# One table word in place of two for TensorE's steps in the building stage of a graph kernel

## The reference

```python
x = x + attention(h, src, dst)          # scores, exp, weighted segment sums, layernorm
x = x + graph_conv(h, src, dst)         # degree-normalised segment sum, one weight
x = x + message_mlp(h, edge_attr, ...)  # two edge MLPs, segment sums to both ends
x = x + gated(h, src, dst, edge_type)   # four GRU steps over segment_sum(msgs, dst)
```

## Time and profile before

| | |
|---|---|
| median of 3 runs | 15553.18 us (15549.36 to 15561.5) |
| the profiled execution | 15585.08 us, span 15583.4 us |
| tables, until the first step | 332 us |
| building stage | 3702 us |
| attention to the end | 11549 us |
| TensorE busy over the span | 72% |

### The profile page before, as it was taken

How to read it: one execution, slowest core, us unless ns; L and a number is a source line. 1 busy time by engine, 2 the same in 40 slices (tenths; PEclk the granted TensorE clock), 3 DMA queues, 4 the chain that set the end, 5 groups by cost and what they waited for, 6 DMA issues and landing times.

```text
span 15583.4 us, 278381 instructions
## 1 busy us (share of the span) xinstructions
PE 11255.6 (72%) x60408; PEld 6377.3 (41%) x60409; DVE 6103.9 (39%) x28509; ACT 3526.9 (23%) x9549; POOL 4597.2 (30%) x4343
## 2 busy tenths in 40 slices
PE   2444444444699976677677677777669999999999
PEld 2222222222222235555555555555554444444443
DVE  6667666766444424333333333333330000000000
ACT  0333333333222202222222222222210000000000
POOL 2000000000000006888888888888800000000000
PEclk7665665665699988999999999999959999999999
DMA  2222222222211152333333333333359989899888
GB/s 92 88 87 87 87 87 91 87 87 87 84 67 71 71 240 36 41 41 41 41 41 41 41 42 41 42 41 41 41 51 345 342 332 341 322 349 342 331 339 305
DMA packets 1120442, 2096.49 MB, mean 135 GB/s; under 512 B 372941, under 2 KB 982880, under 8 KB 1012496
## 3 DMA queue, kind: packets, MB, share of 16 engines
q1 hardware_dynamic: 823736, 1913.57, 34.9%
q0 software_dynamic: 295904, 174.34, 10.9%
HBM read 1630.27 MB, written 457.23 MB: 134 GB/s over the span
## 4 chain that ended last, share of the span: by engine, by line
PE 45%; issue 25%; POOL 14%; DVE 10%; ACT 2%; DMA 1%; DVEq 1%; SPq 1%; POOLq 0%; another core or an unknown queue 0%; ACTq 0%
PE ps L1465 14%; POOL G L488 7%; PE ps L1470 7%; PE ps L1127 7%; POOL reverse L811 5%; DVE hots L1790 3%; PE ps L1182 2%; PE ps L1173 2%; DVE hots L1788 2%; DVE hots L1789 2%; DVE weighed L1864 1%; PE ps L1407 1%; ACT expo L860 1%; DMA reverse<-SD,sidx 1%; PE ps L1268 1%
## 5 line engine op out<-in xcount | busy, mean ns | idle before, releaser
L1127 PE MATMUL ps<-hots 128*128 128x392 f16 x4859 | 1698.6, 453 | 2003.8 <-issue 1751.6
L811 POOL DMA_INDIRECT reverse<-SD,sidx x1660 | 2653.7, 1599 | 389.5 <-issue 380.5
L1465 PE MATMUL ps<-chunk,feat 128*128 128x512 f16 (+1 forms) x10192 | 2279.0, 375 | 14.4 <-DVE feat L2136 13.5
L841 ACT ACTIVATE stagebuf<-ps 128x392 f32 x3248 | 1447.3, 504 | 2288.9 <-PE ps L1130 2234.2
L488 POOL DMA_INDIRECT G<-h_table,idx x1660 | 1652.5, 995 | 493.0 <-issue 484.4
L1127 PEld LDWEIGHTS ps<-hots 128*128 128x128 f16 x4859 | 640.9, 132 | 2779.3 <-issue 2699.8
L1990 DVE TENSOR_TENSOR acc<-acc,ps 128x132 f32 x1660 | 485.4, 292 | 3147.1 <-PE ps L1331 3049.5
L1328 PE MATMUL ps<-MS,OH 128*128 128x128 f32 x3320 | 779.0, 318 | 1263.7 <-issue 791.1
L1788 DVE TENSOR_SCALAR hots<-count_lo,key_lo 128x128 f16<-128x128 f16 x4859 | 1196.0, 246 | 1127.4 <-PE ps L1130 1127.4
L1465 PEld LDWEIGHTS ps<-chunk,feat 128*128 128x128 bf16 x10192 | 943.1, 98 | 1342.7 <-issue 349.5
L1790 DVE TENSOR_SCALAR hots<-count_hi,key_hi 128x294 f16<-128x294 f16 x4859 | 1410.9, 290 | 0.0
(11 more groups left out here) (413 smaller groups left out, 15175.6 us busy)
## 6 DMA issues: line engine op xcount, KB each, us to landing
chunk<-adj SPq DMA_DIRECT2D x720, 1792.0 KB, 9.0
adj<-stagebuf SPq DMA_DIRECT2D x406, 784.0 KB, 5.3
chunkA<-adj SPq DMA_DIRECT2D x48, 1792.0 KB, 6.7
chunk<-adj SPq DMA_DIRECT2D x60, 1232.0 KB, 6.4
G<-in_edge SPq DMA_DIRECT2D x1660, 32.0 KB
G<-h_table,idx POOLq DMA_INDIRECT x1660
reverse<-SD,sidx POOLq DMA_INDIRECT x1660
reverse<-acc SPq DMA_DIRECT2D x4, 3225.0 KB, 20.0
```

The source lines that it names most:

```text
L811: nc.gpsimd.indirect_dma_start(reverse[j % R], bass.IndirectOffsetOnAxis(sidx[:, j:j + 1], 0), SD[:, j % R, :], None, compute_op=ALU.add). ...
L841: nc.scalar.activation(stagebuf[:, bass.ds(held["word"][j] >> ENDBITS, SLEN)].rearrange("p (x c) -> p x c", c=BLK)[:, :, 0:2], bank[j % 8] ...
L1127: nc.tensor.matmul(ps[:, bass.ds(held["to"][j % STEPW], 2 * COMBS)], hots[:, j % BRING, 0:P], hots[:, j % BRING, P:P + 2 * COMBS], start=F ...
L1465: nc.tensor.matmul(bank[k % 2][:, 0:cols], feat[0][:, hi, 0:2, :].rearrange("p a d -> p (a d)"), columns(chunk4, i % DRING, m, cols), star ...
```

## The change

The bank of the step and the bank to clear are put in one word of row 32: the bank to clear times 4096, plus the bank of the step. TensorE loads 4 and 16 words at the start of an iteration in place of 4, 16 and 16. It takes the word apart at each step: `& 7 * 512` gives the bank of the step, `>> 12` the bank to clear. The counts keep their row 0. VectorE fills the third part of `tabcols` with zeros, and makes the sum with two instructions in place of one.

```diff
-                if j % STEPW == 0:
-                    held["to"], held["clear"] = words(32, k, STEPW, 1, 7 * 512), words(64, k, STEPW, 1, 7 * 512)
+                    held["banks"] = words(32, k, STEPW, 1, 7 * 512 * 4097)
...
-                nc.tensor.matmul(ps[:, bass.ds(held["to"][j % STEPW], 2 * COMBS)], hots[:, j % BRING, 0:P],
+                nc.tensor.matmul(ps[:, bass.ds(held["banks"][j] & 7 * 512, 2 * COMBS)], hots[:, j % BRING, 0:P],
...
-                nc.tensor.matmul(ps[:, bass.ds(held["clear"][j % STEPW], 1)], zero16[:, :], zero16[:, 0:1],
+                nc.tensor.matmul(ps[:, bass.ds(held["banks"][j] >> 12, 1)], zero16[:, :], zero16[:, 0:1],
...
-            copy_(tabcols[:, 2 * BC:3 * BC], i1).then_inc(tab_cols, 1)
+            link(nc.vector.memset(tabcols[:, 2 * BC:3 * BC], 0.0))
+            link(copy_(f0, i1))
+            both_(out=tabcols[:, BC:2 * BC], in0=f0, scalar=4096.0, in1=tabcols[:, BC:2 * BC], op0=ALU.mult,
+                  op1=ALU.add).then_inc(tab_cols, 1)
```

## The result

| | before | after |
|---|---|---|
| median of 4 runs | 15557.34 us (15549.36 to 15565.15) | 15193.28 us (15191.78 to 15195.78) |
| ratio, 95% interval | | 0.9766 (0.9751 to 0.978) |
| span of the profiled execution | 15583.4 us | 15191.1 us |
| first load to last clearing matmul | 328.2 to 4034.1 | 329.1 to 3659.9 |

The change takes 364 us away, and 15193 lies in the range of 15150 to 15325. The two profiled executions differ by 392 us. Of that, 375 us are in the building stage and 18 in all that follows. I don't count the second part as work of the change: what follows the stage took between 11524 and 11552 us in the profiled executions of all kernels of this document whose stores are whole, and 11527 in one whose building stage differs from before in the ring alone. The profiled execution of before was 28 us above its own median, that of after was at its median.

What follows compares the result with a forecast made beforehand. The building stage was taken to be bound by a ring of waits between TensorE and VectorE; -497 (load) + 188 (register work) - 20 (stores) + 0.4 (table) = -329 us took 15553 to 15224 us, range 15150 to 15325.

Steps and rivals of the forecast that it cites:

- What bounds the stage: Building stage: a ring of waits through TensorE's loads, first step, VectorE's eight hots and last batch, 10.8 us undisturbed.
- The load: Start of each iteration: removing the third load and its gap saves 1.635 us, 497 us in all; escaped stores 20 more.
- Its length: Remaining 16-word load: 1.11 or 1.28 us undisturbed; taken to belong to the table's row, 52 us kept for the range.
- the rival with 15296 us: The last load keeps the longer time and no store is escaped; 52 and 20 us fall away; chance 0.14.
- The register work: TensorE's first step and last batch: mask 0.10 us, shift 0.03, together 0.62 us an iteration, 188 us.
- The covered steps: Eleven steps between first step and last batch: cost nothing, hidden by VectorE's hots, with 0.35 us left.
- The slower case: Register work breaks the cover from 0.16 us a step; at 0.25 a loss of 168 us, 15721 us; chance 0.05.
- The clock: TensorE keeps 2.4 GHz through the shorter load pause; first step gains 48 us at most, 15176 us; chance 0.12.
- The locked stores: Stores meet the two remaining loads more often, which inherit 56 us, and 20 us are not had: 15300 us; chance 0.07.
- The table: VectorE's table, ahead of all that follows: two instructions more, 0.4 us once.
- The signs: Trace marks: 608 loads, undisturbed iterations every 9.97 us, VectorE's wait about 800 us, TensorE's "issue" about 1300.
- The rule that spoke for a larger gain: Register loads at about 200 ns a register: 3.2 us for 16 words, change worth 833 us; not used in the sum.

Runs made afterwards that it cites:

- kernels with small stores: Before and after, each with building-stage stores of one seventh of their bytes; stage 3283 us in before, 2982 in after, one run each.
- ring of 16: Before and after, each with 16 hots buffers in place of 8: 15146.69 and 15144.67 us.
- one-word kernel: After with count, bank and bank to clear in one word, one 16-word load an iteration: 14817.53 us with 8 buffers, 14816.69 with 16.
- count-with-clear word: After with the bank to clear moved into the count's word, no mask on the step's bank: 15078.21 us with 8 buffers, 14781.67 with 16.

## Why the prediction was right, point by point

**What bounds the stage.** Right. The ring stands in after with the same links, and VectorE's saved wait of 377 us is the stage's gain.

**The load.** I took 1.635 us an iteration and 20 us for stores, 517 us. Measured was 1.83, or 556. The step "undisturbed it takes 1.28 us, the gaps about 0.17" held (1.281 and 0.16). The 20 us for escaped stores were too many: the two loads that stayed lose 1.18 us an iteration to stores where they lost 1.20, some 7 us over the stage. With the 56 us of stores that were in the third load itself (445.3 - 304 x 1.28) it is 63. That 56 + 20 comes so near the 75 us of the kernels with small stores is luck. What the sum lacked is the first load, which fell from 1.167 to 0.994 us when the third went. That term was zero in the working and is 52 us. It needed a trace with two loads.

**Its length.** "I take it to belong to the row of the table" was right: the load of row 32 kept 1.101 us as the last one and 1.102 as the first, so the rival with 15296 us fell.

**The register work.** 0.62 us an iteration, measured 0.58 (0.61 by means). A mask of 0.10 is 0.09; a shift of 0.03 is 0.04. The mask in the first step takes its 0.09 too, but shows as 0.05, since before lost 0.045 us at this place by itself. A mask stands also ahead of the last batch's first step, behind the wait, with 0.09. The clearing instruction takes 73 ns where I expected about 67.

**The covered steps.** Zero was right, with a smaller margin than I gave: the sequencer alone needs 5.03 us from first to last batch, by the ring of 16, not 4.92, against 5.28. The third batch already came late, 0.42 us behind its hots in place of 0.14, which cost nothing, since the fourth waited for VectorE. This is the step on which the sign hung. The pair with 16 buffers shows what is there without it: 2 us of gain in place of 364. The sign that I had named, over 5.3 us from first to last batch, was missed by little: it is 5.27 in the iteration above and 5.28 in the median.

**The slower case** had its mechanism right and its price not reached. Its threshold was 0.16 us a step more. By the measured 3.44 and 5.28 us it is 0.15. After lies under it with 0.13 a step (5.03 less 3.44, over 12) and keeps its cover; the one-word kernel lies over it with 0.17, and there the last batch came 0.16 us late by its register instruction.

**The clock.** The granted clock of the stage is 0.62 after 0.61, and in 96% of the iterations the first step still ends 0.5 us after its weights (2197.48 to 2197.99). The shorter pause, 2.85 to 3.1 us in undisturbed iterations, against 4.45 in that of the earlier trace rows, didn't keep the higher level. So this rival gave at most 4% of its 48 us, 2 us. The Trainium skill (TensorE: Matmul & The Clock Gate, What's actually happening) has the throttled state as the default, and the 0.62 here agrees.

**The locked stores** fell. The two loads that stayed lose 0.85 + 0.33 = 1.18 us an iteration to stores, in before they lost 0.89 + 0.31 = 1.20. They inherited nothing.

**The table.** 0.4 us was right: from the first cast into `tabcols` to the next comparison behind the table it is 1.00 us in before (209.05 to 210.05) and 1.40 in after (210.31 to 211.71). The first load of the stage comes 0.97 us later in after, but that is not the table's price, for in the other kernels it comes anywhere from 322.8 to 329.5.

**The sum.** Loads and gap 556, register work 0.58 x 303 = 176: 380 against my 329, and 375 in the trace. Between the medians it is 364, 11 less than the stage gained in the trace; the runs of before spread over 16 us (15549 to 15565). So I had 35 us too little gain, on a median of before that was 4 us too low: 31 us in all. The forecast came that near because the parts that I had were the right ones; the largest error is the 52 us of the first load, and the 13 us too many for the stores took some of it back.

**The signs.** Line 1112 has its 608 loads, and those of over 3 us fell from 121 to 99, though as a share they rose from 13% to 16%. Undisturbed iterations take 9.8 us where I had 9.97, for the first load. VectorE's wait is 750.5 us where I had 800. TensorE's "issue" is 886.4 and not 1300, but with the pauses put down to VectorE's hots it is 1314.5.

**The rule that spoke for a larger gain** stays contradicted. The Trainium skill (Runtime: NRT & Kernel Launch, Instruction fetch mechanics) has about 200 ns for each register even in bulk; it gives that in speaking of the runtime's own register loads, and these read a table in SBUF. Here 4 words take 0.99 or 1.17 us, 16 take 1.10 and 32 take 2.13, 67 to 69 ns a word at the last two.

## What to carry to other kernels

Draw the ring of waits and ask of each register instruction whether it stands on it: the same masks and shifts cost 0.58 us an iteration here with eight buffers and 2.12 with sixteen, and the gain went from 364 to 2 us. Try the cheap way to open a ring first: sixteen buffers alone gave 412 us. Pack table words until a load holds 16, for 4 words cost nearly as much as 16 here; beyond that measure before doubling. And try edits together: the count-with-clear word is worth 115 us over after with eight buffers, and 363 over after with sixteen.

## What was not expected of the hardware

- A register load of 4 words spread over 13 takes 0.994 us in kernels with two loads an iteration and 1.167 in those with three. Row 64's load is longer than row 32's by 0.172 us, the same amount. Whether it is one cause stays open; it was not tried.
- 16 words take 1.10 us and 32 take 2.13. Steps of size between them were not measured.
- A store that holds the DMA engines makes a load of 16 words last up to 3.9 us, and one of 32 up to 5.5. Over the stage the full stores cost before 423 us, 11% of it, 406 of them in the loads: more than the change was worth.
- A mask on TensorE's sequencer is a record of 32 ns, but the next instruction starts 0.09 us after it, three times as much. Its length is no measure of what it costs.
- With the same instructions, the first step's address instruction starts 0.297 us behind the last load in before, and 0.252 in before with small stores or a ring of 16. It does so in nearly every iteration. The cause is open.
